# Perceiver with six layers on one core: the weighing of the odd slots moved ahead of their scores and maxima

## The reference

```python
qh = (q @ Wq + bq).reshape(B, LQ, HEADS, D_K).transpose(0, 2, 1, 3)
kh = (k @ Wk + bk).reshape(B, LKV, HEADS, D_K).transpose(0, 2, 1, 3)
vh = (v @ Wv + bv).reshape(B, LKV, HEADS, D_K).transpose(0, 2, 1, 3)
scores = jnp.einsum('bhqd,bhkd->bhqk', qh, kh) * scale
attn = jax.nn.softmax(scores, axis=-1)
out = jnp.einsum('bhqk,bhkd->bhqd', attn, vh)
...
x = x + _L0_xattn_ref(_layernorm(x, axis=-1), ctx_512, ctx_512, ...)
```

## Time and profile before

| | |
|---|---|
| median of 3 runs | 1417.14 us (1416.73 to 1419.59) |
| the profiled execution, its own time | 1416.92 us |
| its span | 1415.1 us |
| TensorE matmul busy | 1357.3 us (96%) |
| VectorE busy | 1071.3 us (76%) |
| ScalarE busy | 960.0 us (68%) |
| GpSimd busy | 287.2 us (20%) |

### The profile page before, as it was taken

One profiled execution on the slowest core, in us unless ns is written; L12 is line 12 of the kernel. 1 busy time (PEld: TensorE's weight loads), 2 busy tenths in 40 slices (PEclk: granted clock), 3 DMA queues, 4 the chain that ended last, 5 costly groups with the idle time before them and its releaser, 6 DMA issues.

```text
span 1415.1 us, 32674 instructions
## 1 busy us (share of the span) xinstructions
PE 1357.3 (96%) x13282; PEld 793.4 (56%) x13282; DVE 1071.3 (76%) x2114; ACT 960.0 (68%) x1997; POOL 287.2 (20%) x321
## 2 busy tenths in 40 slices
PE   7799999999999999999999999899999999989998
PEld 4244555444555444555444545457557999856666
DVE  4777787888787888787888888725876768767757
ACT  5367787877788777888777666753796654348731
POOL 3344222212212222212223000000003100001110
PEclk9799999999999999999999999998999999999999
DMA  6846454345454345454345522001402320356000
GB/s 177 190 135 160 118 138 110 75 115 137 107 139 111 71 119 137 105 138 114 70 109 160 131 46 46 2 15 47 120 24 64 110 66 1 93 122 147 1 1 30
DMA packets 98791, 134.55 MB, mean 95 GB/s; under 512 B 11024, under 2 KB 74128, under 8 KB 92688
## 3 DMA queue, kind: packets, MB, share of 16 engines
q1 hardware_dynamic: 98640, 132.45, 37.4%
HBM read 94.15 MB, written 38.27 MB: 94 GB/s over the span
## 4 chain that ended last, share of the span: by engine, by line
PE 86%; DVE 7%; ACT 5%; issue 1%; DMA 1%; SPq 0%; POOL 0%; ACTq 0%; DVEq 0%; POOLq 0%
PE psum L553 19%; PE psum L573 17%; PE psum L534 7%; PE psum L606 4%; PE psum L2182 4%; PE psum L2156 3%; PE psum L653 3%; PE psum L1276 2%; PE psum L2901 2%; DVE peaks L714 2%; ACT probs L812 2%; PE psum L613 2%; PE psum L1673 1%; PE psum L275 1%; PE psum L2911 1%; PE psum L2864 1%
## 5 line engine op out<-in xcount | busy, mean ns | idle before, releaser
L714 DVE TENSOR_REDUCE peaks<-psum 128x1 f32<-128x512 f32 x1024 | 656.1, 686 | 157.5 <-PE psum L534 147.7
L812 ACT ACTIVATE probs<-psum 128x512 f32<-128x512 f32 x1024 | 556.3, 596 | 181.0 <-PE psum L553 170.2
L553 PE MATMUL psum<-queriesT,keysT 64*128 64x256 bf16 (+1 forms) x4096 | 332.6, 274 | 16.6 <-ACT probs L812 16.1
L553 PEld LDWEIGHTS psum<-queriesT,keysT 64*128 64x128 bf16 (+1 forms) x4096 | 166.3, 95 | 210.7 <-ACT probs L812 167.2
L573 PE MATMUL psum<-probs,values 128*17 128x256 f32 x4096 | 271.7, 383 | 0.0
L534 PE MATMUL psum<-keysT,queriesT 64*128 64x512 bf16 x1024 | 211.1, 381 | 8.6 <-DMA keysT<-key_parts 4.9
L573 PEld LDWEIGHTS psum<-probs,values 128*17 128x17 f32 x4096 | 94.2, 96 | 128.0 <-issue 77.8
L962 POOL CAST key_parts<-key_f 128x512 bf16<-128x512 f32 x57 | 34.7, 609 | 494.9 <-ACT key_f L851 452.0
L534 PEld LDWEIGHTS psum<-keysT,queriesT 64*128 64x128 bf16 x1024 | 59.9, 95 | 31.5 <-DVE peaks L714 18.9
L606 PE MATMUL psum<-ctxT,wk 128*128 128x256 f32 x192 | 67.1, 431 | 0.2 <-DVE peaks L714 0.2
L968 POOL TENSOR_TENSOR key_parts<-key_r,key_parts 128x512 bf16<-128x512 f32 x57 | 65.9, 1157 | 4.6
(11 more groups left out here) (321 smaller groups left out, 1739.3 us busy)
## 6 DMA issues: line engine op xcount, KB each, us to landing
keysT<-key_parts SPq DMA_DIRECT2D x186, 256.0 KB, 5.8
key_parts<-key_parts SPq DMA_DIRECT2D x90, 256.0 KB
ctx_nat<-in_ctx_dram SPq DMA_DIRECT2D x32, 256.0 KB, 3.2
ctx_in<-in_ctx_dram SPq DMA_DIRECT2D x24, 256.0 KB, 4.7
ctx_turned<-ctxT SPq DMA_DIRECT2D x24, 256.0 KB, 6.2
ctx_T<-ctx_turned SPq DMA_DIRECT2D x12, 512.0 KB, 4.0
qk_parts<-early_weights SPq DMA_DIRECT2D x24, 128.0 KB
q_parts<-q_parts SPq DMA_DIRECT2D x20, 128.0 KB
```

The costliest lines, as they stand in the source:

```text
L553: made = e.matmul(ps[j][:, e2 * S:(e2 + 1) * S], self.keysT[own, plane, i % RING, kt * P:(kt + 1) * P], self.queriesT[own, plane, u % 2, g ...
L714: e.tensor_reduce(self.peaks[:, i % 2, j * QT + qt, c:c + 1], k.ps(("max", n)), AX.X, ALU.max).then_inc(*self.peaked.up(n))
L812: e.activation(self.probs[:, t % RINGP, 2 * j * S:(2 * j + 2) * S], k.ps(("scores", t, j)), ACT.Exp).then_inc(*self.exped.up((t, j)))
```

## The change

In `tensor`, the block that does the weighing of an odd slot is written ahead of that slot's scores and maxima; before, it was written behind them. The even slots are as they were, as are the waits inside the block, the other engines' programs and the table of jobs. The lines below it move by one, so the scores are line 553 before and 572 after, the weighing 573 before and 553 after, and a job's line is one less.

```diff
         for t in range(FIRST, TOTAL + 3):
+            if t % BLOCK == 1 and BLOCK + 1 <= t <= TOTAL + 1:
+                i, p0 = divmod(t - BLOCK - 1, SLOTS)
+                b, g = divmod(i, NG)
+                w.wait_ge(self.exped, (t - 2, 1))
+                for p in range(p0, p0 + BLOCK):
+                    w.wait_ge(self.v_kept, (b, p))
+                w.wait_ge(self.ones_set, b % 2)
+                if i:
+                    w.wait_ge(self.outT_kept, i - 1)
+                w.wait_ge(self.cleared, 0)
+                for p in range(p0, p0 + BLOCK):
+                    for e2 in range(2):
+                        for j in range(GH):
+                            quad, half, kt = e2 * GH + j, 2 * j + e2, 2 * p + e2
+                            made = e.matmul(k.bank(SUMS)[32 * quad:32 * quad + DH + 1, 0:S],
+                                            self.values[b % 2][:, kt, g * GH + j, :],
+                                            self.probs[:, (SLOTS * i + p) % RINGP, half * S:(half + 1) * S],
+                                            start=(p == 0), stop=(p == SLOTS - 1))
+                made.then_inc(*self.weighed.up((t - BLOCK - 1) // BLOCK))
             maxima = self.maxima(t)
...
             for n in maxima:
                 find_max(n, t)
-            if t % BLOCK == 1 and BLOCK + 1 <= t <= TOTAL + 1:
...
-                made.then_inc(*self.weighed.up((t - BLOCK - 1) // BLOCK))
-
             for job, *a in self.due.get(t, ()):
```

## The result

The changed kernel takes 1502.58 us in the median (1500.22 to 1506.32, 4 runs), against 1416.93 us before in the same comparison (1415.45 to 1419.59). The ratio is 1.0605, with a 95% interval of 1.0575 to 1.0635: slower by 86 us. The prediction was 1524 us with a range from 1503 to 1545. Direction and mechanism came as forecast, the single stall was shorter than forecast, and the median lies 0.4 us under the range.

A forecast was written before the change was run, and what follows sets the result against it. TensorE was taken to bound the slots. Stalls of 0.58 us in net 196 pairs, +113.7 us, less 7 us from VectorE, gave +107 us on the profiled 1415.1 us span, with 1.8 us around it: 1524 us, range 1503 to 1545.

The forecast's parts named there:

- The bound: In the 512 slots TensorE sets the time, busy 688 us of the first 695; ScalarE and VectorE are not full.
- The mechanism: With only maxima between two score blocks, the second waits for ScalarE to free head 0's bank: some 230 waits, about 100 us.
- The price of one place: Each pair whose score blocks have only maxima between them costs 0.58 us more, read from one such place before.
- the net 196 places: Pairs in the slots that newly get the stall, 210, less 13 that lose it; at 0.58 us each, 113.7 us.
- The neighbourhood of job and weighing: On TensorE, whether a weighing behind a job is dearer than behind maxima; claimed no extra cost.
- So nothing for that: The same job takes 1.93 us to the next start with scores behind it, 1.92 with a weighing: zero added.
- Rival 3: On TensorE the stall comes, but job and weighing side by side save one layout switch: 1506 us, chance 0.08.
- VectorE's give-back: Longer pairs let VectorE catch up at group ends, so maxima lose 0.27 us of delay in about 27 groups: 7 us saved.
- ScalarE's slack: ScalarE finishes exponentials and eviction at 3.48 us, before the next odd scores at 4.40: 0.9 us spare, so the stall doesn't grow.
- rival 4: ScalarE falls behind on bunched exponentials and evictions: up to 1618 us, likelier 1540 to 1550, chance 0.08.
- The sum: Over the kernel, 113.7 us for the stalls less 7 us from VectorE: +107 us.
- The range's lower end: 1503 us for the whole kernel; the lower bound worked out was 1506, one 0.09 us step saved in 196 pairs, 18 us.

The follow-up runs named there:

- e1: The changed kernel with the even slot's job ahead of its scores on TensorE, weighing still first in odd slots: 1449.18 us, ratio 1.0262 to the kernel of before.
- e5: e1 with the even slots' jobs also ahead of the exponentials on ScalarE and the reduces on VectorE: 1403.29 us, ratio 0.9925 to the kernel of before.
- e6: The changed kernel with a fourth bank for the scores, taken from the four of the maxima and jobs: 1540.64 us, ratio 1.0895 to the kernel of before.
- e3: The changed kernel with the even slot's maxima ahead of its scores, so four maxima lie between the score blocks: 1457.15 us, ratio 1.0319 to before.
- e4: The changed kernel with a second, long fulfilled wait ahead of the odd slots' first exponential on ScalarE: 1514.85 us, ratio 1.0724 to the kernel of before.
- e8: The changed kernel with the shift's transposes ahead of the even slot's other job, away from the weighing: 1507.31 us, ratio 1.0657 to the kernel of before.

## Why the prediction was wrong, and where it was right

**The bound.** Right. The slots grew by 87 us and the stretch behind them by 0.4.

**The mechanism.** Right, and tested from both sides. The scores wait 234 times in place of 37, 85 us in all, where some 230 and about 100 us were forecast. Put a job between the score blocks (e1, e5) and the waits go, wherever the weighing stands. Give the scores a fourth bank (e6) and they go too, over to VectorE. Fill the wait (e3) and the block ends at the same time.

**The price of one place: the term that was mis-sized.** "The second block takes 762.40 - 761.36 = 1.04 us instead of 0.46." In the changed kernel it takes 0.98. The step that failed is the transfer from the earlier trace rows to the new places: that row exposes the first exponential of an even slot, which has two waits on ScalarE, the change exposes that of an odd slot, which has one. e4 shows the 0.06 us by adding the wait, and gets 14 us for some 230 places. In the sum, the net 196 places cost 12 us less, and some 27 of the old ones, which turn from even to odd exponentials, 1.6 us less. The trace of before had both lengths; I quoted one and did not ask why the other places were shorter.

**The neighbourhood of job and weighing.** "So nothing for that" holds for float32 jobs: 0.63 us from keys to weighing as to scores. It does not hold for the shift's transposes, 0.11 us less in 24 groups, 2.6 us (e8). Rival 3 was right for this one kind of job.

**VectorE's give-back.** Right: 7 us forecast. Before, the maxima held TensorE up 28 times for VectorE, 7.0 us in all; after, 3 times, 2.0 us.

**ScalarE's slack.** Right: rival 4 did not come. The stall is the same in all slots of a group.

**The sum.** 107 - 12 - 1.6 - 2.6 = 91 us, against 87 for the profiled slots and 90 for the kernels at like clock. The 4 us between 91 and 87 sit in the first slots and are no work of the change. The first scores start at 65.17 us before and 67.83 after, and the granted clock is 0.50 there in both, the lower level of 1.2 GHz. The kernel of before:

```profile
72.00:74.00 2.00, 2.00 (x23) 0.75 (x14) 0.58 (x1) 0.00 (x0) 0.00 (x0) 0.50 0.52 199
74.00:76.00 2.00, 2.00 (x10) 0.61 (x6) 1.27 (x2) 1.10 (x3) 0.00 (x0) 0.73 0.52 202
```

The mean of 0.73 over the last stretch puts the rise to the upper level at about 75.1 us; TensorE is busy all through both stretches. The changed kernel, with its first weighing:

```profile
68.00:70.00 2.00, 1.82 (x19) 0.94 (x16) 0.67 (x2) 1.64 (x3) 1.23 (x2) 0.68 1.01 201
70.00:72.00 2.00, 1.63 (x25) 0.82 (x23) 2.00 (x5) 1.77 (x5) 1.85 (x3) 1.00 0.58 188
71.60 1.06 PE L553 MATMUL psum<-probs,values 128*17 128x256 f32 x16
```

Here the clock rises at about 69.3 us. So the slots of before ran 9.9 us at the lower level and those of the changed kernel 1.5, and at half the clock the 8.4 us more are worth up to 4.2 us of TensorE's time. It is not the new order that brought the clock up: the first block that the change moves starts at 71.60, behind the rise. Why the rise comes earlier in one execution than in another is open.

**The range.** With the 0.06 us and the transposes in the sum, 1524 would have been 1508, and the changed kernel took 1506.32 us at the clock of the profile that the sum starts from. That execution and one more (1504.46 us) lie inside the range, and the two at 0.992 lie under it: that the median fell 0.4 us under it, and not inside, is the luck of the clock. The forecast itself was 18 us over at like clock, and 16 of them are the terms above. The range's lower end came from one further switch of layout saved, 18 us; that another part of the price could be smaller at the same time was not in it.

## What to carry to other kernels

When two producer blocks share a short ring of banks, ask what stands between them in the queue and not how many switches the order has: here a switch of 0.09 us was saved, and the pair became 0.52 us longer. Lay the long blocks so that each gap between two of them covers the consumer's time, and give each filler's bank back in the order in which it is handed out, on every engine. A place in the old trace with the neighbourhood that the change makes is the best price there is, but take it from the instance that has the same waits.

## What the runs showed of the hardware

- A wait that is long fulfilled, but is the second on an instruction of ScalarE, moved its start by 0.06 us where it stood right behind the event it was really waiting for (from 0.65 to 0.71 us behind the scores' start, e4).
- Two blocks on TensorE whose matmuls use narrow column strips, 2 and 17 columns, overlap where they meet: the weighing's first matmuls start 0.01 us after the transposes' first. The step from maxima to float32 work takes 0.09 us more than from maxima to scores (0.31 against 0.22 us).
- ScalarE's exponentials are recorded 0.60 us long, but two in a row take 1.08 us together.
- In the kernel of before, single executions whose mean granted clock was 0.985 to 0.987 took 1415.60 to 1417.86 us, and those at 0.991 to 0.994 took 1408.48 to 1412.45 us.
